# High parts of the norms' columns made by ACT, and the mix placed behind the first transposes

## The reference, cut

```python
sa = _mha(x, x, x, tgt_mask, ...)                      # 16 heads of 16: softmax(q k' / 4) v, then @ wo + bo
x = _ln(x + sa, ln1_g, ln1_b)
ca = _mha(x, enc_output, enc_output, memory_mask, ...) # queries from x, keys and values from the context
x = _ln(x + ca, ln2_g, ln2_b)
ff = jax.nn.relu(x @ ff_w1 + ff_b1) @ ff_w2 + ff_b2    # 256 -> 1024 -> 256
x = _ln(x + ff, ln3_g, ln3_b)
```

## The kernel before, in words

| step | X (behind turn 0) | Y (behind turn 1 and the mix) | behind turn 2 | behind turn 3 |
|---|---|---|---|---|
| x0 | `ff.pe_hidden` 6 | `proj2.pe_q` | ff out, `proj2.pe_v` | `att2.pe_out` |
| x1 | `proj1.pe_k` | `norm2.pe` | ff out twice | ff out, `ff.pe_hidden` 0 |
| y0 | `proj1.pe_q` | `ff.pe_hidden` 2 | ff out, `proj1.pe_v` | ff out, `att1.pe_out` |
| y1 | `proj2.pe_k` | `norm1.pe` | ff out, `ff.pe_hidden` 4 | ff out, `norm3.pe` |

## Time and profile before

### The profile page before, as it was taken

How to read it: one execution, slowest core, us unless ns; L and a number is a source line. 1 busy time by engine, 2 the same in 40 slices (tenths; PEclk the granted TensorE clock), 3 DMA queues, 4 the chain that set the end, 5 groups by cost and what they waited for, 6 DMA issues and landing times. The chain is left out here.

```text
span 3718.2 us, 79408 instructions
## 1 busy us (share of the span) xinstructions
PE 3191.6 (86%) x27248; PEld 2726.8 (73%) x27248; DVE 2138.0 (58%) x4222; ACT 1879.8 (51%) x7766; POOL 1654.9 (45%) x2020
## 2 busy tenths in 40 slices
PE   8999996899999997379999999737999999966887
PEld 5998995688888887267877777626888888754664
DVE  2555553444444444357777777525777777744665
ACT  2444442334333333256666666425676666634775
POOL 1223221024444445235666666622566666662544
PEclk8999998999999998689999999968999999988999
DMA  3111112110111110211112111021111111103331
GB/s 105 51 51 65 59 37 105 57 37 24 48 48 48 48 46 32 105 47 55 52 57 61 56 57 54 21 102 41 49 49 53 53 55 55 41 29 100 93 97 54
DMA packets 192554, 213.62 MB, mean 57 GB/s; under 512 B 30208, under 2 KB 161536, under 8 KB 189696
## 3 DMA queue, kind: packets, MB, share of 16 engines
q1 hardware_dynamic: 192384, 211.40, 17.9%
HBM read 131.59 MB, written 58.72 MB: 51 GB/s over the span
## 5 line engine op out<-in xcount | busy, mean ns | idle before, releaser
L1641 ACT ACTIVATE second_stage<-second_psum,second_neg_max 128x128 f32<-128x128 f32 x1024 | 362.9, 392 | 245.7 <-DVE second_neg_max L1621 245.5
L1641 ACT ACTIVATE third_stage<-third_psum,third_neg_max 128x128 f32<-128x128 f32 x1024 | 362.5, 388 | 224.4 <-DVE third_neg_max L1621 224.3
L1641 ACT ACTIVATION_READ_ACCUMULATOR second_stage<-second_psum,second_neg_max 128x1 f32 x1024 | 237.5, 232 | 0.0
L1641 ACT ACTIVATION_READ_ACCUMULATOR third_stage<-third_psum,third_neg_max 128x1 f32 x1024 | 233.8, 228 | 0.0
L534 POOL TENSOR_TENSOR cross_ff_hidden_lo<-cross_ff_relu,cross_ff_hidden_hi 128x256 fp32r<-128x256 f32 x128 | 93.2, 729 | 289.4 <-DVE cross_ff_hidden_hi L529 289.4
L1621 DVE TENSOR_REDUCE second_neg_max<-second_psum 128x4 f32<-128x512 f32 x256 | 169.2, 684 | 61.9 <-PE second_psum L1584 60.2
L1621 DVE TENSOR_REDUCE third_neg_max<-third_psum 128x4 f32<-128x512 f32 x256 | 168.8, 682 | 41.8 <-PE third_psum L1584 40.7
L1524 ACT ACTIVATE fourth_stage<-fourth_psum,fourth_neg_max 128x128 f32<-128x128 f32 x512 | 181.8, 386 | 3.5 <-DVE fourth_neg_max L1500 3.5
L1595 PE MATMUL third_psum<-third_eye,third_stage 128*128 128x128 f32 x1024 | 163.2, 283 | 15.7 <-DVE third_p_turned_odd L1627 7.9
L1595 PE MATMUL second_psum<-second_eye,second_stage 128*128 128x128 f32 x1024 | 162.4, 282 | 14.7 <-DVE second_p_turned_odd L1627 7.5
L529 DVE CAST cross_ff_hidden_hi<-cross_ff_relu 128x256 fp32r<-128x256 f32 x128 | 44.9, 351 | 212.4 <-ACT cross_ff_relu L524 212.4
(11 more groups left out here) (438 smaller groups left out, 12637.7 us busy)
## 6 DMA issues: line engine op xcount, KB each, us to landing
second_stage<-second_a_k SPq DMA_DIRECT2D x512, 16.0 KB, 1.8
third_stage<-third_a_k SPq DMA_DIRECT2D x512, 16.0 KB, 1.8
cross_arena<-in_l0b_packed SPq DMA_DIRECT2D x6, 1024.0 KB, 4.9
self_arena<-in_l0a_packed SPq DMA_DIRECT2D x4, 1024.0 KB, 6.3
self_x_raw<-in_x_t SPq DMA_DIRECT2D x8, 512.0 KB, 3.7
self_x_rows<-in_x_rows SPq DMA_DIRECT2D x8, 512.0 KB, 3.8
self_ct_raw<-in_ctx_t SPq DMA_DIRECT2D x8, 512.0 KB, 4.3
context_hi<-self_ct_hi SPq DMA_DIRECT2D x8, 512.0 KB, 4.9
```

Source lines behind the costliest of these rows:

```text
L1641: ins = act.activation(self.sh.p_wide[:, 4 * b + t, x, :], psum[:, SCORE_BANKS[t], x * SEQ:(x + 1) * SEQ], ACT.Exp, bias=self.sh.neg_max[: ...
```

## The change

Two things, both in `second` and `third`. First, the cast that makes the high part of a norm's columns leaves DVE's queue for ACT's, directly behind the activations that make the columns (`act_hi`). The subtraction stays on DVE (`dve_lo`), at its place for `norm1` and `norm2`; for `norm3` it moves from ahead of `proj2.dve_v` to behind the last `turned` of x0. Second, in each of the four steps PE does `mix(before)` directly behind turn 0, ahead of X, where it stood ahead of Y; ACT's `spread` moves ahead of the reading out of X's bank, and DVE's `norm(before)` ahead of `turned` 1 and the fourth maximum.

```diff
@@ -1739,11 +1739,15 @@
                                  ACT.Identity, bias=self.shift[:, k:k + 1], scale=self.gain[:, k:k + 1])
         ins.then_inc(self.turned_ready.sem, 1)
 
-    def dve_split(self, dve, r, stored=None):
+    def act_hi(self, act, r, stored=None):
+        if stored is not None:
+            act.wait_ge(stored.sem, stored.at(r, 0))
+        act.wait_ge(self.turned_ready.sem, self.turned_ready.at(r, 1))
+        act.copy(self.yt.hi[:], self.y[:]).then_inc(self.hi_ready.sem, 1)
+
+    def dve_lo(self, dve, r, stored=None):
         if stored is not None:
             dve.wait_ge(stored.sem, stored.at(r, 0))
-        dve.wait_ge(self.turned_ready.sem, self.turned_ready.at(r, 1))
-        dve.tensor_copy(self.yt.hi[:], self.y[:]).then_inc(self.hi_ready.sem, 1)
         dve.wait_ge(self.hi_ready.sem, self.hi_ready.at(r, 1))
         dve.tensor_tensor(self.yt.lo[:], self.y[:], f32(self.yt.hi[:]),
                           ALU.subtract).then_inc(self.lo_ready.sem, 1)
@@ -2154,45 +2158,48 @@
 
                 if ok(-4):
                     norm3.act(act, Back(r, 4), psum)
+                    norm3.act_hi(act, Back(r, 4), stored)
                 exp(x0_next, 0)
+                spread(x0)
                 if ok(-3):
                     ff.act_relu(act, Back(r, 3), psum, 6)
                 exp(x0_next, 1)
-                spread(x0)
                 if ok(-1):
                     proj2.act_q(act, Back(r, 1), psum)
                 exp(x0_next, 2)
                 exp(x0_next, 3)
 
                 exp(x1_next, 0)
+                spread(x1)
                 if ok(1):
                     proj1.act_k(act, Back(r, -1), psum)
                 exp(x1_next, 1)
-                spread(x1)
                 if ok(-2):
                     norm2.act(act, Back(r, 2), psum)
+                    norm2.act_hi(act, Back(r, 2))
                 exp(x1_next, 2)
                 exp(x1_next, 3)
 
                 if ok(-2):
                     ff.act_relu(act, Back(r, 2), psum, 0)
                 exp(y0_next, 0)
+                spread(y0)
                 if ok(1):
                     proj1.act_q(act, Back(r, -1), psum)
...
                 exp(y1_next, 0)
+                spread(y1)
                 if ok(0):
                     proj2.act_k(act, r, psum)
                 exp(y1_next, 1)
-                spread(y1)
                 if ok(0):
                     norm1.act(act, r, psum)
+                    norm1.act_hi(act, r)
                 exp(y1_next, 2)
                 if ok(-2):
                     ff.act_relu(act, Back(r, 2), psum, 4)
...
@@ -2262,17 +2269,17 @@
                 turned(x0[1], 0)
                 maximum(x0[2], 1)
                 maximum(x0[2], 2)
+                norm(x0[0])
                 turned(x0[1], 1)
                 if ok(-3):
                     ff.dve_hi(dve, Back(r, 3), 6)
                 maximum(x0[2], 3)
-                norm(x0[0])
                 turned(x0[1], 2)
-                if ok(-4):
-                    norm3.dve_split(dve, Back(r, 4), stored)
                 if ok(-1):
                     proj2.dve_v(dve, Back(r, 1), psum)
                 turned(x0[1], 3)
+                if ok(-4):
+                    norm3.dve_lo(dve, Back(r, 4), stored)
 
                 if ok(-2):
                     norm2.dve_sum(dve, Back(r, 2), psum, norm1.rows_ready, norm2.scaled)
...
@@ -2440,10 +2447,10 @@
 
                 scores(x0[2])
                 turn(x0[1], 0)
+                mix(x0[0])
                 if ok(-3):
                     ff.pe_hidden(pe, Back(r, 3), banks, 6)
                 turn(x0[1], 1)
-                mix(x0[0])
                 if ok(-1):
                     pe.wait_ge(norm1.lo_ready.sem, norm1.lo_ready.at(Back(r, 1), 1))
                     proj2.pe_q(pe, Back(r, 1), banks, norm1.yt)
...
                 scores(x1[2])
                 turn(x1[1], 0)
+                mix(x1[0])
                 if ok(1):
                     pe.wait_ge(layer.x_loaded.sem, layer.x_loaded.at(Back(r, -1), 32))
                     proj1.pe_k(pe, Back(r, -1), banks, xt)
                 turn(x1[1], 1)
-                mix(x1[0])
                 if ok(-2):
                     norm2.pe(pe, Back(r, 2), banks)
```

More of the change, by code:

```diff
@@ L2182, in body @@
                 exp(y0_next, 1)
-                spread(y0)
                 if ok(-2):
@@ L2285, in body @@
                 maximum(x1[2], 2)
+                norm(x1[0])
                 turned(x1[1], 1)
                 maximum(x1[2], 3)
-                norm(x1[0])
                 turned(x1[1], 2)
                 if ok(-2):
-                    norm2.dve_split(dve, Back(r, 2))
+                    norm2.dve_lo(dve, Back(r, 2))
                 turned(x1[1], 3)
@@ L2304, in body @@
                 maximum(y0[2], 2)
+                norm(y0[0])
                 turned(y0[1], 1)
                 maximum(y0[2], 3)
-                norm(y0[0])
                 turned(y0[1], 2)
@@ L2323, in body @@
                 maximum(y1[2], 2)
+                norm(y1[0])
                 turned(y1[1], 1)
                 maximum(y1[2], 3)
-                norm(y1[0])
                 turned(y1[1], 2)
                 if ok(0):
-                    norm1.dve_split(dve, r)
+                    norm1.dve_lo(dve, r)
                 turned(y1[1], 3)
@@ L2476, in body @@
                 turn(y0[1], 0)
+                mix(y0[0])
                 if ok(1):
@@ L2479, in body @@
                 turn(y0[1], 1)
-                mix(y0[0])
                 if ok(-2):
@@ L2493, in body @@
                 turn(y1[1], 0)
+                mix(y1[0])
                 if ok(0):
@@ L2497, in body @@
                 turn(y1[1], 1)
-                mix(y1[0])
                 if ok(0):
```

## The result

The changed kernel took 3732.4 us in the median of its runs (3723.2 to 3738.5), the kernel before 3714.7 beside it: ratio 1.0045, 95% interval 1.0031 to 1.0059. It is **slower by 0.45%**, 17 us; I had forecast 3706.5, faster by 0.26%. The profiled execution took 3733.5 us with a span of 3731.8, against 3719.9 and 3718.2.

The account below looks back on a forecast made before the run. PE bounds the kernel, through its stops and the low clock behind them. Full rounds +5.2 us, drain -1.7 and clock -13.3 sum to -9.8: forecast 3706.5 us, 0.26% faster, range for 8 in 10 3693 to 3727.

Parts of the forecast that it names:

- x0: forecast -1.50 + 0.68: End of x0: dve_v no longer waits behind norm3's split, -1.50 us a round; the bare handover to Y adds 0.68.
- the handover of 0.74: PE's wait between X and Y for ACT's read-out, 1.10 less turn 1's 0.36; taken as 0.68 us in x0 and y0.
- x1: forecast -0.31: Step x1 in second: norm2's subtraction no longer beside POOL's residual, 0.77 instead of 1.66 us; about -0.31 a round.
- y1: forecast +0.81: Step y1: ACT's later k delays the columns by 0.77 us; with the new cast, about 0.81 in all.
- The clock: PE's clock falls in steady rounds of both phases cost 16.6 us; four fifths come back, -13.3 us.
- the long stop: PE's wait for dve_v at the end of x0, 1.91 us idle, to fall to about 0.6.
- A: Rival: the same number of rounds keeps the low clock; 3719.7 us, no change; chance 0.22.
- B: Rival: six short stops a round lower PE's clock in every round; 3734 us, slower; chance 0.09.
- D: Rival: no handover cost between X and Y, so the gains stand alone; 3660 us; chance 0.05.
- "While the pipeline drains ... -1.7 us": Drain of both phases: the mix fills waits for ACT's columns, 0.4 us four times, -1.7 us; bounds 0 and -5.
- Rival C: ACT becomes the chain in y1, a round longer by 0.4 to 0.8 us; 3716 to 3726 us; chance 0.14.
- the 0.6 of `hidden` 4: Step y1, profile after: PE's ff.pe_hidden 4 waits 0.6 us for the columns.

Follow-up runs that it names:

- order alone: Kernel before with only mix, norm and spread moved, all splits on DVE at their old places; 3763.96 us, ratio 1.0137.
- `dve_v` first: Kernel before with one edit: norm3's split, both halves on DVE, behind the last turn of x0; 3662.25 us, ratio 0.9867.
- residual late: Kernel before with norm3's split behind the last turn of x0 and POOL's residual behind the reciprocals of y0; 3640.27 us, ratio 0.9809.

## Why the prediction was wrong

**Terms of a steady round of `second`**, before to after by the step table. x0: forecast -1.50 + 0.68 = -0.82, measured -0.77. y0: forecast +0.68, measured +0.75; the 0.06 that I took off the handover of 0.74 was not there. x1: forecast -0.31, measured -0.31. y1: forecast +0.81, measured **+1.04**. Of that the move is 0.87 (the order alone) where I had 0.77, and the cast 0.17, just the 0.55 - 0.38 of the forecast. The rest failed by my own rounding: 0.77 + 0.55 - 0.38 is 0.94, and I wrote "less rounding, about 0.81". Together +0.71 against +0.36. In `third` it was +0.62 against +0.07: y1 again, and x1 gained about 0.45 of the forecast 0.60. Over 12 rounds each, +16 us instead of +5.2.

One reading behind x1 was wrong, and cost nothing. I wrote that POOL is silent beside the subtraction of 0.77 us in y1 (2101.35). It was making the mask flags:

```profile
2101.01 1.04 POOL L1845 TENSOR_SCALAR second_mask_flags<-second_mask_ints 128x256 bf16<-128x256 int32 x1
```

With POOL silent the subtraction takes 0.69, as in x1 of the changed kernel, where the later start (0.66 instead of 0.55) took that back.

**The clock.** Forecast: four fifths of 16.6 us back. Measured: no steady round below 1.00, so all of the 17 us that those 22 rounds had in the profile (555.1 - 11 x 49.45 = 11.2, and 537.6 - 11 x 48.34 = 5.9; by these intervals 6 rounds of 11 in `third` were such, not 6 of 10). The mechanism was right: the falls went with the long stop, and six stops of 0.5 us in a round made none. Rivals A and B are refuted for the steady rounds, D by the handovers of 0.74, and with B the rule of the Trainium skill (TensorE: Matmul & The Clock Gate, section A second HAM failure mode: psum-queue depth-cycling) does not come true here: the short stops left the clock at 1.00. But the long stop does not always bring a fall: with the order alone it stays at 1.8 us, and 10 of 11 rounds of `second` have 1.00, 8 of 11 of `third` 0.97.

**"While the pipeline drains ... -1.7 us"** is the step that failed most. I looked for the places where the move could help in incomplete rounds, and bounded it by 0 and -5, with no loss. The runs show +14 (by the ratios) to +21 (by the medians). The gain of the change exists only where `norm3`'s split and `dve_v` both exist, 13 rounds of a phase, 4 to 16. The price of the move falls in the other rounds, the drain and the start of the next phase as well. In two places the clock is seen lower beside the longer waits (0.50 behind the stop of 3.38 us, 0.75 against 0.83 in the start of `third`). In rounds 0 and 1 it stays open what the move costs and what the clock.

**The sum.** Steady rounds about +16 - 17 = -1, ends +14 to +21: +13 to +20, against the 17 measured. Rival C (ACT's chain in y1) had the right place, with 0.23 a round above the forecast where it had 0.4 to 0.8, but not the reason: the cast took 0.62 and not 1.05, and cost y1 the 0.17 of the forecast. That the cast costs x1 another 0.21 beside the moved mix I did not see. Of what the profile after was to show, the waits for ACT, the 0.6 of `hidden` 4 (0.51), the cast and the subtraction came as written, and the rounds of 50.2 stayed below the 50.5 at which I would have called it wrong. I had written 49.9 for them, and 48.4 for those of `third`, which took 48.96. That was no guard, since the loss lay outside the rounds that I had named.

**The bigger gain beside it.** The forecast had named both stops and priced the first right: its -1.50 a round over 24 rounds, alone, with the clock's 17, is 53 us, and `dve_v` first gives 49 (by the ratio) to 54 (by the medians). The change spends them on the move.

## What to carry to other kernels

When a software pipeline is reordered, count gain and price in the incomplete rounds separately: a gain may exist only in full rounds while its price is paid in all, here 14 to 21 us. Before an operation is moved, write down what it covers where it stands (here, ACT's read-out of the bank between two pieces), and what stands behind it in the queues of the other engines that move with it (here, DVE's copy of a turn behind the norm). An edit that is free in one order need not be free in another: the casts on ACT cost nothing with the mix at its old place and 0.4 us a round with it moved. And price each half of a change for itself: the half that removed the stop was worth 1.3% with one edit, and with the work moved that lay beside the next stop it became 1.9%.

## What the hardware showed

Times of one operation on 128x512, from and to SBUF (float32 in, fp32r out):

| operation | POOL idle | beside a POOL operation |
|---|---|---|
| cast on DVE | 0.43 (order alone, 2087.05) | 0.59 beside the end of a 128x256 one (residual late, 2043.77), 1.51 beside 128x512 |
| subtraction on DVE | 0.69 (residual late, 2044.40) | 0.77 beside the mask flags (before, 2101.35), 1.64 to 1.66 beside 128x512 |
| cast on ACT | 0.62 (2083.35 in the changed kernel) | 0.62 (0.617 to 0.626 over all 96 of the changed kernel) |

So DVE's cast is the faster one when POOL is idle, and by far the slower one beside a large POOL operation. Moving the POOL operation by a few us was worth 22 us of the kernel. The clock in the first rounds of a phase differs between two kernels with the same order of work there, by some 4 us in an interval; single profiles do not settle differences of that size.
